# Input-row scatters issued one at a time: two attention layers and two expert layers on one core

## The reference, cut to what matters

```python
x = x + attn_a(layernorm(x))      # 8 key heads, 4 query heads each, head size 8, causal, rotary
x = x + moe(layernorm(x))
x = x + attn_b(layernorm(x))      # differential attention, 16 heads
x = x + moe(layernorm(x))         # the same weights again

def moe(xt):                      # xt: 2048 rows of 256
    scores = softmax(xt @ Wg.T)                       # 16 experts
    # the best 2 of 4 groups of experts, then the best 4 experts in them
    combine = zeros(T, 16); combine[t, topi] += scores[t, topi]
    h = silu(xt @ W1[e].T) * (xt @ W3[e].T)           # inner size 176, for each expert e
    y = sum over e of combine[:, e] * (h @ W2[e].T)
    z = (silu(xt @ Ws1.T) * (xt @ Ws3.T)) @ Ws2.T     # shared expert, inner size 352
    return y + z
```

## Time and profile before

| | |
|---|---|
| time, median of 2 runs | 1459.29 us (1458.84 to 1459.74) |
| span of the profiled execution | 1458.9 us |
| mean granted clock of PE | 0.898 of full speed |
| PE busy | 1153.4 us (79%) |
| DVE busy | 873.6 us (60%) |
| POOL busy | 689.3 us (47%) |
| ACT busy | 543.1 us (37%) |
| input-row scatters, L672 | 128, 123.3 us on POOL, 963 ns each |
| result scatters, L688 | 80 and 80, 125.0 and 124.7 us on POOL |

### The profile page before, as it was taken

The page is one execution under the profiler, slowest core; times in us unless marked ns, Lnnn a source line. Parts: engine busy times, 40 slices in busy tenths (PEclk is TensorE's granted clock), DMA queues, the critical chain, the costliest instruction groups (busy, mean ns, idle before and its releaser), DMA issues.

```text
span 1458.9 us, 25835 instructions
## 1 busy us (share of the span) xinstructions
PE 1153.4 (79%) x8690; PEld 619.8 (42%) x8690; DVE 873.6 (60%) x2061; ACT 543.1 (37%) x846; POOL 689.3 (47%) x841
## 2 busy tenths in 40 slices
PE   6878999887862399999468899998788227999990
PEld 2333334334631256665244344443275114666650
DVE  5688899853740135555389799998478002455543
ACT  2226677686400012222122477777841001222210
POOL 4443345442067216677563354444502760467771
PEclk9978999999895699999789899999988658999995
DMA  4325556304522148888655321221071322688868
GB/s 150 116 80 180 180 181 191 119 17 147 151 93 106 68 118 152 146 153 147 126 176 166 119 56 55 57 56 32 24 246 38 108 93 78 141 149 150 154 98 248
DMA packets 154353, 177.42 MB, mean 122 GB/s; under 512 B 20016, under 2 KB 139760, under 8 KB 153712
## 3 DMA queue, kind: packets, MB, share of 16 engines
q1 hardware_dynamic: 124336, 136.38, 31.3%
q0 software_dynamic: 29184, 38.36, 15.5%
q10 hardware_dynamic: 704, 1.02, 0.2%
HBM read 91.12 MB, written 83.78 MB: 120 GB/s over the span
## 4 chain that ended last, share of the span: by engine, by line
PE 55%; DVE 18%; another core or an unknown queue 7%; issue 7%; ACT 5%; DMA 4%; SPq 3%; POOL 1%; POOLq 0%; ACTq 0%; DVEq 0%
PE pair_ps L1963 11%; PE o_ps L1734 7%; DVE nm L1103 4%; PE pair_ps L1996 4%; ACT arena L829 3%; DVE bm L1103 3%; PE pair_ps L1999 2%; PE pair_ps L1906 2%; PE t_ps L1760 2%; PE pair_ps L1684 2%; PE pair_ps L1565 2%; PE pair_ps L1970 2%; DMA arena<-mT 2%; PE pair_ps L1659 2%
## 5 line engine op out<-in xcount | busy, mean ns | idle before, releaser
L829 ACT ACTIVATE arena<-pair_ps 128x1024 f32<-128x1024 f32 x320 | 323.4, 1024 | 137.4 <-PE pair_ps L1659 80.2
L614 POOL TENSOR_SCALAR_AFFINE_SELECT arena<-arena 128x512 f32<-128x512 f32 (+1 forms) x320 | 175.7, 549 | 249.0 <-ACT arena L829 248.5
L1103 DVE TENSOR_REDUCE nm<-pair_ps 128x2 f32<-128x1024 f32 (+1 forms) x192 | 232.6, 1222 | 40.4 <-PE pair_ps L1708 36.9
L672 POOL DMA_INDIRECT x_slots<-y_sb,slot_i x128 | 123.3, 963 | 154.0 <-DVE slot_i L1310 115.6
L1734 PE MATMUL o_ps<-arena 128*9 128x512 f32 (+7 forms) x2048 | 179.5, 446 | 4.3 <-POOL arena L614 4.1
L688 POOL DMA_INDIRECT y_h<-xnT,dest x80 | 124.7, 1559 | 107.6 <-DVE xnT L1453 83.6
L688 POOL DMA_INDIRECT y_f<-xnT,dest x80 | 125.0, 1562 | 105.5 <-DVE xnT L1453 80.4
L1963 PE MATMUL pair_ps<-arena 128*128 x512 | 167.0, 467 | 3.1 <-issue 1.7
L1103 DVE TENSOR_REDUCE bm<-pair_ps 128x8 f32<-128x1024 f32 x128 | 155.3, 1217 | 5.7 <-PE pair_ps L1708 2.7
L1916 PE MATMUL t_ps<-arena,hw 128*128 128x256 f32 (+1 forms) x96 | 30.2, 443 | 123.4 <-DVE x_sb L1399 77.5
L1436 DVE TENSOR_TENSOR arena<-arena,pair_ps 128x128 f32<-128x128 f32 x144 | 41.5, 288 | 127.4 <-ACT arena L885 88.1
(11 more groups left out here) (273 smaller groups left out, 2078.5 us busy)
## 6 DMA issues: line engine op xcount, KB each, us to landing
arena<-x_slots SPq DMA_DIRECT2D x128, 132.5 KB
arena<-in_w SPq DMA_DIRECT2D x4, 2816.0 KB, 18.8
x_slots<-hw SPq DMA_DIRECT2D x19, 530.0 KB, 3.6
arena<-q_a SPq DMA_DIRECT2D x64, 96.0 KB
arena<-q_b SPq DMA_DIRECT2D x64, 96.0 KB
y_f<-hw SPq DMA_DIRECT2D x11, 512.0 KB, 4.1
y_h<-hw SPq DMA_DIRECT2D x11, 512.0 KB, 4.1
arena<-in_w SPq DMA_DIRECT2D x2, 2048.0 KB, 17.1
```

What stands on the lines that cost most here:

```text
L614: pool.affine_select(p, p, pattern, ALU.is_ge, 0.0, base=0, channel_multiplier=-1)\
L672: pool.indirect_dma_start(x_slots, bass.IndirectOffsetOnAxis(ap=slot_i[:, t, k:k + 1], axis=0), y_sb[:, t, :], None).then_inc(sm("scat0" i ...
L829: act.activation(p_ring[:, U % RING, :], pair_ps[:, pair_at("T", n, u)].rearrange("p a c -> p (a c)"), ACT.Exp, scale=SCALE).then_inc(sm(" ...
L1103: dve.tensor_reduce(dst, src, X, ALU.max, negate=not 2 <= u < 4).then_inc(sm("t_max_done"), 1)
```

## The change

Every input-row scatter but the first of a layer gets a wait ahead of it. In the first 40 of a layer, scatter `n` waits until `scat0` holds the 16 of each of the `n` scatters before it; scatter 40 waits for all 40 of `scat0`; those after it wait for the scatters before them on `scat1`. `past` adds what the first layer left on the semaphore, in the second layer.

```diff
             def scatter(n):
                 t, k = n // TOPK, n % TOPK
+                early = EARLY_T * TOPK
+                if 0 < n <= early:
+                    pool.wait_ge(sm("scat0"), 16 * (n + past(f, early)))
+                elif n > early:
+                    pool.wait_ge(sm("scat1"), 16 * (n - early + past(f, NT * TOPK - early)))
                 pool.indirect_dma_start(x_slots, bass.IndirectOffsetOnAxis(ap=slot_i[:, t, k:k + 1], axis=0),
                                         y_sb[:, t, :], None).then_inc(sm("scat0" if t < EARLY_T else "scat1"), 16)
```

## The result

The changed kernel takes 1549.28 us, the median of 2 runs (1547.25 to 1551.31), against 1459.29 us: a ratio of 1.0603 with a 95% interval of 1.0563 to 1.0644. It is 90 us slower, 28 us more than forecast and inside the forecast range. The profiled execution has a span of 1549.6 us against 1458.9, and a mean granted clock of 0.875 against 0.898.

A forecast was written before the change was run, and what follows sets the result against it. The path was taken to go through the silence during POOL's scatters and the shared part behind it. Serialized scatters would block result scatters: 1458.9 + 31.9 + 30.3 = 1521.1, so 1521 us, range 1485 to 1565.

The forecast's parts named there:

- the silence: First expert layer: DVE hears of PE's matmul 65 us late while scatters go out; forecast to leave the path, 8 us won at most.
- the ring of 8: DVE's ring `yt`: scaling tile 8 needs result scatter 0 landed; tile 9 +31.9 us in the first layer, +30.3 in the second.
- the period: POOL's scatters, start to next start: 1.27 us before, 2.7 us after, with floor 2.36 and ceiling 3.67.
- meetings: Scatters running beside SP's tile loads: 0.5 us on each of 11, 5.5 us a layer; bounds nothing and 24 us.
- the 0.39 us from packets to landing: Part of the period: from the last result scatter's packets to SP's issue, SP's own waking included.
- the waking of 0.29 us: Part of the period: time to wake POOL; the sum 2.75 was taken as 2.7 us, as the 0.39 holds a waking.
- The first tile load: SP's first load after the 40th scatter lands: between 508 and 520; experts begin near 516.5 instead of 524.37.
- The new wait: DVE behind the last scatter: result scatter 0 follows by 1.27 us, lands 3.98 later; tile 9 comes 1.87 after tile 8.
- The clock: PE restarts at the lower clock level after its second pause; nothing charged, bound 2 us a layer.
- The floor of 2.36 us a scatter: Rival for POOL's scatters: landing follows packets at once, nothing collides; 1467 us, chance 0.11.
- the ring does not bind: Rival: only the 40th scatter counts, each layer wins 8 us; 1443 us or a little less, chance 0.03.
- the silence comes from scatters as such: Rival: the silence stays, not depending on scatter density; experts begin near 620, 96 us late; 1650 us, chance 0.08.

The follow-up runs named there:

- two in flight: Against the changed kernel, scatter n waits for the landing of scatter n-2, with two semaphores taking turns; 1373.47 us, ratio 0.9407.
- 320 cleared columns: Against the changed kernel, no scatter waits for a landing; POOL clears 320 columns of a free tile between two scatters; 1368.35 us, ratio 0.9363.
- bursts of eight: Against the changed kernel, only every eighth scatter waits, for all scatters before it; 1378.71 us, ratio 0.9434.
- 160 columns: Against the changed kernel, no scatter waits for a landing; POOL clears 160 columns of a free tile between two scatters; 1425.09 us, ratio 0.9742.

## Why the prediction was right, and where it was off

*The mechanism* was right in each step: the silence vanished (the table after 3.83 us of waiting, the shared part over at 456.9 where "about 456" was forecast), the ring of 8 took its place, and one pause of 37.72 us on PE in the first layer ends behind the landings of result scatters 0 and 1. The experiments hold up both halves: spacing alone removes the silence, and taking the result scatters out from behind the others removes the pause of 38.66 us at tile 8.

*The size* was 28 us too small, 62 us forecast against 90, and one term makes it: **the period**. The range held the time because its upper end allowed 2.95 us and 11.5 us of meetings a layer. Forecast were 2.7 us and 5.5 us of meetings a layer, 175.6 us from the first to the last scatter; it took 592.07 - 403.41 = 188.7 us, and 1351.29 - 1160.87 = 190.4 us in the second layer. The first 40 starts span 113.95 us, 2.92 us each, and no tile load is under way there. The last 24 take 74.7 us, 3.11 us each. The meetings with tile loads therefore cost 24 x 0.19 = 4.6 us, near the 5.5 charged; they fall, as charged, on the scatters that run while tiles are loaded (13 periods of 3.31 us from 520.17 to 563.22), and the 10 behind them go 2.89 us apart. The base was 0.22 us too low, 63 times. The step that failed is the 0.39 us from packets to landing, read from the last 4 packets of one quiet result scatter, and the waking of 0.29 us, which I left half out. Start to landing measures 2.4 at the least, 2.6 at the median and up to 4.8 us, so the quietest scatters are what I forecast (2.07 + 0.39 = 2.46; the shortest period of the layer is 2.67 us) and the mean is not. A mean of waits that lie in series takes in the tail, which one sample cannot show. Adding the full waking to the median gives 2.9 us, and that would have been the sum to make.

The Trainium skill, "DMA: Bandwidth & Descriptors", section "Anatomy of one DMA — SWDGE (gpsimd) path", gave an estimated 2.31 us from start to landing. The trace disagrees: no landing was under 2.4 us, and the median is 2.6.

*The first tile load* was forecast between 508 and 520 and went at 520.92; PE began at 523.32, not 516.5. That is the same term over 39 periods, 8.6 us, less 1.8 us by which this execution's scatters began earlier.

*The new wait* behind the last scatter was right to a tenth: the result scatter followed by 1.27 us, and tile 8 was scaled 3.91 us after it started (3.98 forecast), tile 9 1.92 us later (1.87). In the first layer tile 9 comes at 599.17, +43.2 us against 31.9 forecast. In the second layer it comes at 1358.37 against 1268.83, +89.5; the layer's first scatter stood 44.5 us late, so +45.0 against 30.3.

*The clock* was charged at nothing with a bound of 2 us a layer. The granted clock was 0.52 over PE's first 66 us without work and 0.55 over its pause, near the lower of its two levels (1.2 of 2.4 GHz), and 0.97 afterwards, with the first group after the pause at 2.07 us. From tile 9 to the layer's last result scatter (759.35 against 715.01) the delay grows from 43.2 to 44.3 us; 1.2 us more is found in the second layer. With these the sum closes: 1458.9 + 43.2 + 1.1 + 45.0 + 1.2 = 1549.4, measured 1549.6.

*The rivals.* The floor of 2.36 us a scatter fell: the shortest period is 2.67 us. That the ring does not bind fell with the waits of 38.66 and 40.06 us. That the silence comes from scatters as such fell with the changed kernel, and more sharply with two in flight and with 320 cleared columns.

What stays open is what holds PE's news back while POOL issues scatters 1.27 us apart. It is not all news. In the middle of the silence of the kernel before, ACT starts at 439.77 on a product that PE ended at 421.41, but DVE follows ACT, and PE follows DVE, within 0.1 us:

```profile
439.77 0.59 ACT L876 ACTIVATE sil<-pair_ps 96x512 f32<-96x512 f32 x1 [23.00 <-issue]
```

```profile
440.40 0.68 DVE L1411 TENSOR_TENSOR hw<-sil,pair_ps 96x512 f32<-96x512 f32 x1 [20.04 <-issue]
```

```profile
441.14 2.07 PE L1916 MATMUL t_ps<-arena,hw 96*128 96x256 f32 x4 [14.47 <-issue]
```

One rival is untested: the recording itself. Every execution here was recorded, and the recording loses events where the silence is. Of the 1024 increments with which the 64 scatters of the first layer land, the trace holds all 1024 in the changed kernel, 707 with 320 columns, 596 with two in flight, 361 with bursts of eight, 213 with 160 columns, and 150 in the kernel before. Either both have one cause, or the recording holds the engines up; no run here is without it. The runs show a rate at which the silence begins, and that rows, packets and the number on their way are not its measure; they don't show the place.

## What to carry to other kernels

Where waits for a landing are put in series, the mean period counts: start to landing at the median, plus the waking, plus a tail, and not the quietest sample. Before a stream of transfers is slowed down, look at what stands behind it in the same engine's queue and which ring of buffers that feeds: here the order in the queue cost 18 us a layer. And where an engine waits tens of us for news that was long sent, try the spacing of what is issued meanwhile: 0.25 us more between scatters made this kernel 6% faster, and 1.7 us more made it 6% slower.

## What the runs showed of the hardware

In these recorded executions, while POOL issues indirect scatters 1.20 to 1.27 us apart, news of PE's finished matmuls reaches DVE and ACT late, by tens of us after the first ten to twenty scatters (in the kernel before, ACT is on time at 416.17 and late by 18 us at 439.77), while news from ACT to DVE and from DVE to PE takes under 0.1 us. In the expert stage SP's loads are slow to go out as well (7.03 us for two in place of 1.97). At 1.39 us apart PE's news is late in part, and at 1.52 us, or in bursts of eight with stops, the shared part runs on time. Half the rows in a scatter don't help, and the number on their way (two or three) matters only through the spacing. POOL needs 0.89 us for a scatter of 64 rows and 0.96 us for one of 128, so the time is nearly all a fixed part.
